# Dimension-major queries and keys for two narrow attentions, carried by DRAM into the rows that the scores contract over

## The reference

```
# block 4, self: 32 query heads, 8 key/value heads, causal
q = rope(x @ Wq); k = rope(x @ Wk); v = x @ Wv        # rope: first half of a head's 16 dims against the second
p = softmax(mask(q k^T) / 4);  x = layernorm(x + swapaxes(p v) @ Wo)
# block 5, cross: 32 query and 32 key heads over ctx of 256 positions x 256 features
q = axial_rope(x @ Wq, pos); k = axial_rope(ctx @ Wk, pos); v = ctx @ Wv   # even dims against odd dims
w = softmax(q k^T / 4);        x = layernorm(x + (w v) @ Wout + bout)
```

## Time and profile before

| | |
|---|---|
| median of 3 runs | 3688.03 us |
| the profiled execution's own time | 3694.4 us |
| its span, first to last instruction | 3692.8 us |
| TensorE busy over the span | 3308.8 us, 90% |
| VectorE, ScalarE, GpSimd | 2054.9 us, 1347.2 us, 565.8 us |
| mean granted TensorE clock | 0.935 |
| narrow attentions | from 1934.6 us (first weight load) to 2991.9 us (last norm) |

### The profile page before, as it was taken

The page is one execution under the profiler, slowest core; times in us unless marked ns, Lnnn a source line. Parts: engine busy times, 40 slices in busy tenths (PEclk is TensorE's granted clock), DMA queues, the critical chain, the costliest instruction groups (busy, mean ns, idle before and its releaser), DMA issues. The chain is left out here.

```text
span 3692.8 us, 54862 instructions
## 1 busy us (share of the span) xinstructions
PE 3308.8 (90%) x19817; PEld 2544.4 (69%) x19818; DVE 2054.9 (56%) x4982; ACT 1347.2 (36%) x2970; POOL 565.8 (15%) x621
## 2 busy tenths in 40 slices
PE   6999999999999999969937898889898857999995
PEld 6888888888888788854415555555555435787774
DVE  3555665566666666642154665666667645443445
ACT  0444434444444344432113343445445443122110
POOL 1333322222222222014140111210000000000000
PEclk7999999999999999979978999989999978999998
DMA  5111110110011011024340000000000011000001
GB/s 189 52 53 53 52 52 29 35 35 29 30 35 35 29 30 29 1 103 162 135 121 28 2 2 2 23 7 22 5 5 5 2 46 23 24 11 11 23 11 46
DMA packets 110614, 146.77 MB, mean 40 GB/s; under 512 B 23712, under 2 KB 72864, under 8 KB 109288
## 3 DMA queue, kind: packets, MB, share of 16 engines
q1 hardware_dynamic: 95904, 110.80, 9.3%
q0 software_dynamic: 14480, 32.91, 2.9%
HBM read 100.55 MB, written 42.08 MB: 39 GB/s over the span
## 5 line engine op out<-in xcount | busy, mean ns | idle before, releaser
L554 ACT ACTIVATE probs_w<-probs_w,low_w 128x256 f32<-128x256 f32 (+1 forms) x512 | 242.9, 475 | 589.6 <-DVE low_w L599 589.6
L1885 DVE TENSOR_REDUCE mx_n<-bank 128x6 f32<-128x768 f32 (+1 forms) x256 | 279.8, 1093 | 151.1 <-PE bank L1662 80.0
L1793 ACT ACTIVATE probsT_n<-bank 128x768 f32<-128x768 f32 (+1 forms) x256 | 235.7, 921 | 276.1 <-PE bank L1674 275.8
L572 DVE TENSOR_TENSOR probsT_lo_w<-bank,probsT_hi_w 128x384 fp32r<-128x384 f32 (+1 forms) x256 | 159.7, 624 | 124.8 <-ACT probsT_hi_w L537 124.0
L518 PE MATMUL bank<-wo_hi_w,oT_hi_w 128*128 128x512 f32 x512 | 211.6, 413 | 2.1 <-issue 2.1
L1656 PE MATMUL bank<-kT_n,qT_n 48*128 48x256 f32 (+1 forms) x1024 | 124.0, 322 | 93.7 <-DVE mx_n L1885 90.8
L518 PE MATMUL bank<-wo_hi_w,oT_lo_w 128*128 128x512 f32 x512 | 204.4, 399 | 0.0
L518 PE MATMUL bank<-wo_lo_w,oT_hi_w 128*128 128x512 f32 x512 | 204.2, 399 | 0.0
L582 DVE TENSOR_SCALAR probs_w<-probs_w,inv_w 128x256 f32<-128x256 f32 (+1 forms) x512 | 188.6, 411 | 20.8 <-issue 0.9
L450 PE MATMUL bank<-xT_lo_w,wq_hi_w 128*128 128x512 f32 x512 | 161.0, 396 | 0.0
L2323 DVE SCALAR_TENSOR_TENSOR h<-bank,scale_now,silu 128x512 f32<-128x512 f32 x64 | 48.0, 750 | 202.5 <-PE bank L2216 202.5
(11 more groups left out here) (368 smaller groups left out, 8190.3 us busy)
## 6 DMA issues: line engine op xcount, KB each, us to landing
expert_rows<-ctxT_hi_w SPq DMA_DIRECT2D x20, 512.0 KB, 4.5
work_m<-expert_rows SPq DMA_DIRECT2D x40, 256.0 KB, 2.6
expert_products<-work_m POOLq DMA_DIRECT2D x40, 256.0 KB, 2.6
staging_w<-in_L_attn_Wq SPq DMA_DIRECT2D x32, 256.0 KB, 3.0
expert_table<-ctxT_hi_w SPq DMA_DIRECT2D x16, 512.0 KB, 5.5
staging_w<-in_L_attn_Wo SPq DMA_DIRECT2D x32, 256.0 KB, 2.6
staging_w<-in_L_xattn_Wq SPq DMA_DIRECT2D x32, 256.0 KB, 2.7
staging_w<-in_L_xattn_Wo SPq DMA_DIRECT2D x32, 256.0 KB, 2.6
```

The costliest lines, as they stand in the source:

```text
L554: last = act.activation(pr, pr, ACT.Exp, bias=low[:, n % ROUNDS_OF_PROBS, tile:tile + 1], scale=-1.0, accum_out=den[:, n % ROUNDS_OF_PROBS ...
L572: return dve.tensor_tensor(dst, src, hi.bitcast(FP32), ALU.subtract)
L1793: act.activation(probsT[:, turn_ % SLOT_PAIRS, :, 0:cols], scoreT[:, :, 0:cols], ACT.Exp, scale=SCALE)\
L1885: dve.tensor_reduce(to.rearrange("p t h -> p h t"), seen, AX.X, ALU.max).then_inc(s["scores_read"], 1)
```

## The change

Queries and keys are projected with the weights as the stationary operand (`turned`), so that dimensions lie on the partitions and positions along the row, as the scores want them. ScalarE copies the product to `raw`. The rotation's partner dimension is now on the neighbouring partition (the self weights' columns are reordered once by ScalarE so that this holds there too), and SP fetches it with two DMAs to every second partition (`swap`). The tables of cosines and sines are transposed once per cross item (`table`) and once for all self items. VectorE rotates and splits the queries (`split_queries`, five instructions over 128 x 1024), GpSimd the keys (`split_keys`). SP stores both parts to DRAM (`store`, two DMAs each) and reads them back into the contraction rows (`place`, six DMAs of 16 partitions each for queries and for keys). An item is projected and split two iterations ahead and placed one iteration ahead. `parts`, `rotate` and the transposes `kT..`, `qT..` go.

```diff
-    before = [(x, 0) for x in ("xT0", "xT1", "k0", "k1", "kT00", "kT01", "kT10")]
+    before = [(x, 0) for x in ("table", "xT0", "xT1", "k0", "q0", "q1")]
...
+            def swap(name, n):
+                sp.wait_ge(s["prep_act"], uses.nth["q1" if name == "q" else k_uses(n)[-1], n])
+                chunks = DC if name == "q" else dims_chunks(n)
+                for i in range(2):
+                    sp.dma_start(swapped[name][i:P:2, 0:chunks, :], raw[name][1 - i:P:2, 0:chunks, :])\
...
+            def store(name, n):
+                sp.wait_ge(s[f"{name}_split"], n + 1)
...
+                for i, src in enumerate((hi[name].bitcast(FP32), raw[name])):
+                    sp.dma_start(bounce[name][i, 0:chunks, :, :].rearrange("c p t -> p c t"), src[:, 0:chunks, :])\
...
+            def place(name, n):
+                sp.wait_ge(s[f"{name}_stored"], 32 * (n + 1))
+                if n >= 2:
+                    sp.wait_ge(s["scoresT_ready"], 2 * PAIRS * (n - 1))
+                to = (qT if name == "q" else kT)[:, n % 2, :, :].bitcast(FP32)
+                for j, part in enumerate((0, 1, 0) if name == "q" else (0, 0, 1)):
                     for r in range(2):
+                        rows = slice(64 * r + HW * j, 64 * r + HW * j + HW)
...
+            for n in range(-1, ITEMS):
+                if n + 1 < ITEMS:
+                    place("k", n + 1)
+                    place("q", n + 1)
+                if n >= 0:
+                    negatives(1, n)
+                    negatives(2, n)
+                if n + 2 < ITEMS:
+                    swap("k", n + 2)
+                    swap("q", n + 2)
+                if n + 1 < ITEMS:
+                    negatives(0, n + 1)
+                if n + 2 < ITEMS:
+                    store("k", n + 2)
+                    store("q", n + 2)
...
+            def turned(b, n, w, src, chunk, chunks):
+                for cc in range(chunks):
+                    last = pe.matmul(b, w[:, cc, chunk * P:(chunk + 1) * P], src[:, cc, :], start=(cc == 0), stop=(cc == chunks - 1))
...
             def first_scores(n, pair):
-                if pair % 4 == 0:
-                    read(f"qT0{pair // 4}", n)
-                    read(f"qT1{pair // 4}", n)
+                if pair == 0:
+                    pe.wait_ge(s["k_placed"], 96 * (n + 1))
+                    pe.wait_ge(s["q_placed"], 96 * (n + 1))
...
+            def split_keys(n, part):
+                c = dims_chunks(n)
+                a, b, high = raw["k"][:, 0:c, :], swapped["k"][:, 0:c, :], hi["k"][:, 0:c, :]
...
+                if part == 0:
+                    pool.wait_ge(s["prep_act"], uses.nth["table", n if cross(n) else 0])
+                    pool.wait_ge(s["k_swapped"], 32 * (n + 1))
+                    pool.tensor_tensor(a, a, cos, ALU.mult)
...
+            def split_queries(n, part):
+                a, b, high = raw["q"][:, :, :], swapped["q"][:, :, :], hi["q"][:, :, :]
...
+                if part == 0:
+                    dve.wait_ge(s["prep_act"], uses.nth["table", n if cross(n) else 0])
+                    dve.wait_ge(s["q_swapped"], 32 * (n + 1))
+                    dve.tensor_tensor(a, a, cos, ALU.mult)
+                    dve.tensor_tensor(b, b, sin, ALU.mult)
+                elif part == 1:
+                    dve.tensor_tensor(a, a, b, ALU.add)
+                    dve.drain()
+                    dve.tensor_copy(high, a)
                 else:
+                    dve.tensor_tensor(a.bitcast(FP32R), a, high.bitcast(FP32), ALU.subtract).then_inc(s["q_split"], 1)
...
+                    if n + 2 < ITEMS and at in (13, 14, 15):
+                        split_queries(n + 2, at - 13)
```

More of the change, by code:

```diff
@@ L1408, in attention_narrow @@
     key_block = lambda n, h: h // 2 if cross(n) else h // 4
-    turns = lambda n: range(4 if cross(n) else 2)
+    k_uses = lambda n: ("k0", "k1") if cross(n) else ("k0",)
+    dims_chunks = lambda n: kv_heads(n) * HW // P
+    bounce = {name: nc.dram_tensor(f"{name}_parts", (2, DC, P, SEQ), FP32).ap() for name in "qk"}
     GROUPS = ((0, 6), (6, 10), (10, PAIRS))
@@ new lines, in negatives @@
+            def negatives(i, n):
+                name, (lo, hi_) = GROUP_NAMES[i], GROUPS[i]
+                sp.wait_ge(s["prep_act"], uses.nth[name, n])
+                for r in range(2):
+                    for l in range(2):
+                        row, at = 64 * r + ROWS + l, 16 * l + (hi_ - lo) * r
+                        sp.dma_start(qT[row:row + 1, n % 2, lo:hi_, :].bitcast(FP32),
+                                     negT[at:at + hi_ - lo, i, :].bitcast(FP32)).then_inc(s[f"{name}_there"], 16)
@@ new lines, in _ @@
+            for name in "kq":
+                swap(name, 0)
+            for name in "kq":
+                store(name, 0)
+            for n in range(-1, ITEMS):
[13 more added lines that the diff above has]
+                    store("q", n + 2)
@@ L1548, in _ @@
                 .then_inc(s["ctx_loaded"], 16)
[L1550 to L1553, removed]
+            nothing = pool.to_reg(0.0)
             def hide(n, pair):
@@ L1561, in hide, with spread_tables @@
                     .then_inc(s["hidden"], 1)
[L1563 to L1568, removed]
+            def spread_tables(n):
+                if n >= 1:
+                    pool.wait_ge(s["k_stored"], 32 * n)
+                for i in range(2):
+                    for t in range(TILES):
+                        to = spread[:, P * (TILES * i + t):P * (TILES * i + t + 1)].rearrange("p (h w) -> p h w", h=8)
+                        if cross(n):
+                            last = pool.tensor_copy(to, (rotary.cos, rotary.sin)[i][:, batch_of(n) * TILES + t, :]
+                                                    .unsqueeze(1).to_broadcast([P, 8, HW]))
+                        else:
+                            one = chip.const[:, (C_COS, C_SIN)[i] + HW * t:(C_COS, C_SIN)[i] + HW * (t + 1)]
+                            for a in range(2):
+                                last = pool.tensor_copy(to[:, :, a::2], one[:, 8 * a:8 * a + 8].unsqueeze(1).to_broadcast([P, 8, 8]))
+                last.then_inc(s["table_spread"], 1)
@@ L1615, in prepare @@
                     last = four(b, lambda i: ctx_sb[:, i % 2, i // 2 * P:(i // 2 + 1) * P])
+                elif name == "table":
+                    pe.wait_ge(s["table_spread"], max(n - BATCH + 2, 1))
+                    last = four(b, lambda i: spread[:, P * i:P * (i + 1)])
                 elif name in ("k0", "k1"):
@@ L1627, in prepare @@
                         read("xT1", n)
-                        pe.wait_ge(s["wq_cross_loaded" if cross(n) else "wq_loaded"], 16)
-                    last = project(b, xT, int(name[1]), wq, DIM, DC)
-                elif name[0:2] in ("kT", "qT"):
-                    t, n4 = int(name[2]), int(name[3])
-                    pe.wait_ge(s["split"], 4 * n + (0 if name[0] == "k" else 2) + t + 1)
-                    blocks = parts[:, t, :, :].rearrange("p (b two) w -> p b (two w)", two=2)
-                    last = four(b, lambda i: blocks[:, 4 * n4 + i, :])
+                        if cross(n):
+                            pe.wait_ge(s["wq_cross_loaded"], 16)
+                        else:
+                            pe.wait_ge(s["self_turned"], 2)
+                    for i in range(2):
+                        last = turned(b[:, i * SEQ:(i + 1) * SEQ], n, wq, xT, 2 * int(name[1]) + i, DC)
                 else:
@@ L1967, in _ @@
                 do(name, n)
+            for part in range(3):
+                split_queries(0, part)
             for n in range(-1, ITEMS):
```

190 lines of the change are left out of this document (90 added, 100 removed).

## The result

The changed kernel takes 3819.91 us (median of 4 runs, 3815.43 to 3826.95) where the kernel before takes 3690.85 us (4 runs, 3685.89 to 3694.96): the ratio is 1.0345, with a 95% interval of 1.0321 to 1.0368. It is slower by 3.45%, and 3824 us was forecast. The profiled execution has a span of 3825.3 us, 132.5 more than before; its last norm write in the stage stands at 3124.78 us instead of 2991.41, so all of it lies in the narrow attentions.

The account below looks back on a forecast made before the run. TensorE's program order was taken to bound the stage, VectorE close behind. Shorter iterations, outweighed by waits for negatives behind placements, plus start and GpSimd, added 136 us: 3824 us, own range 3750 to 3900, 8-in-10 range down to 3610.

Parts of the forecast that it names:

- The price of a placement: One DMA of 256 KB from DRAM into 16 partitions was put at 2.5 us, 1.25 for self keys.
- The first rival: Placements run at the fast rate, 1.3 us each, so TensorE waits 0.7 and 2 us: 3622 us; chance 0.20.
- the fast row: Lower bound for a placement: 4096 KB to all partitions landed in 20.9 us, 1.3 us per 256 KB.
- The halfway rival: Placements at 1.9 us, negatives at 24.4 (self) and 30.3 us (cross), total 3725 us; chance 0.09.
- SyncE's order: In SP's queue, group B's four negatives DMAs stand behind the queries' store and twelve placements, so they land late.
- The stall, cross: TensorE's wait for group B's negatives at step 6 of a cross iteration: needed at 21, landed at 37.5, 16.5 us.
- Self: The same wait for negatives in a self iteration: needed at 18.5, landed at 30, 11.5 us.
- The sign of 10 to 17 us at pair 6: Profile sign: second scores at pair 6 wait 10 to 17 us for negatives in iterations 0 to 14, more in cross.
- Iterations without DMA trouble: Iteration times from engine work alone: self 60.3 - 7.2 = 53.1 us, cross 66.8 - 9.0 = 57.8 us.
- GpSimd: GpSimd's key splits beside VectorE's norm and split: 2 us in each of six cross iterations, 12 us together.
- The start: First scores at about 1995 instead of 1963.3 us, then 24 instead of 21 us to first second scores: 34 us.
- The swap's wait: Swap issued only after step 11's last query projection: about 1 us of wait beyond step 12, within an unchanged sum.

Follow-up runs that it names:

- half_placed: The changed kernel, with each placement from the third item on carrying only the first half of its heads, same DMAs and order: 3637.55 us, 0.9847 of the kernel before.
- the probe: The changed kernel plus nine groups of four DMAs of about 256 KB into differently placed partitions behind its narrow attentions: 3884.38 us, groups included.
- negb_before_queries: The changed kernel, with SyncE issuing group B's four negatives DMAs between the keys' and the queries' placements: 3667.18 us, 0.9925 of the kernel before.
- half_placed_no_key_split: The kernel with half-size placements, with GpSimd's split of cross items' keys left out but for one tiny instruction: 3619.32 us, 0.9806 of the kernel before.

## Why the prediction was right

The sum, by second scores at the start and norm writes after it; an iteration stands in the distance in which its stall falls:

| | predicted | measured |
|---|---|---|
| start | +34 | +36.4 |
| seven self iterations (0 to 6) | +30 | +33.7 |
| iteration 7 | +9 | +11.0 |
| six cross iterations (8 to 13) | +45 | +46.6 |
| iterations 14 and 15 | +6 | +5.8 |
| GpSimd beside VectorE, cross iterations | +12 | in the rows above |
| together | +136 | +133.5 |

- **The price of a placement**, 2.5 us between 1.3 and 2.6: 2.34 us. The first rival (1.3) fell; half_placed has its time, 3638 against 3622. The reason given, sixteen partitions as an eighth of what the fast row wrote to, is not the right one: the probe shows that it is where they lie and not how many they are. The halfway rival fell too (its 24.4 adds up to 24.6).
- **SyncE's order.** The chain of store, twelve placements and negatives is the one in the timeline. negb_before_queries shows that it decides.
- **The stall, cross:** needed at 21 us (the terms given add up to 21.6), there at 37.5; measured 22.8 and 37.6. **Self:** needed at 18.5, there at 30; measured 21.0 (2208.11 to the stall at 2229.1) and 28.0, a stall of 7.0 us where 11.5 was worked out. The sign of 10 to 17 us at pair 6 came true from iteration 7 on (13.0 to 14.9); in iterations 1 to 6 it was 6.2 to 8.5. The term was too large there, and the self iterations came out right (64.6) by luck: without the stall they are 54.6 us and not 53.1, and a term was missing, since at the lower clock TensorE's matmuls take 4.7 us longer in the self window and 3.4 in the cross window. The working had no clock in it at all.
- **Iterations without DMA trouble:** 53.1 and 57.8 worked out; half_placed has 54.6 and 58.1, half_placed_no_key_split 56.4 for cross. The 53.1 started from 60.3 us, an average with iteration 7 in it; from the 59.8 of the self iterations alone the gain was 5.2 us, not 7.2.
- **GpSimd:** 2 us in each of six iterations worked out; 18 us in all without the stall, 1.7 to 3.3 an iteration. It was counted for too few: keys of cross items are split two items ahead, so iterations 6 and 7 bear it too. The instructions that it holds up most in cross iterations are the norm write's, which have one tensor input and per-row scalars, not two tensors; two inputs in SBUF, as the prediction had it, show in iterations 6 and 7. What it adds in the changed kernel itself, beside the stall, was not measured.
- **The start:** first scores at 1995 worked out, 1994.79 measured; from there to the first second scores 25.9 us instead of 24.
- **The swap's wait** of about 1 us did not show: VectorE's split waited for the swap at the start only.

The mechanism, its place and its price held. That the total came within 4 us is luck in part. GpSimd's 12 us belong to the cross iterations: with them and iteration 7 these were forecast at +66 and measured at +57.6, and all the others, the start included, were forecast at +70 and measured at +75.9. Not tried: a layout in which the sixteen rows lie evenly over the ports (steps of four do, but 48 rows then don't stay together), and a shorter start.

## What to carry to other kernels

Before a small DMA that TensorE waits for is put behind a block of large ones in program order, work out when the block's data end, not when its issues do; moving one call was worth 4% here, and a queue of its own for the small DMA two thirds of that. Ask of a DMA into few partitions where these lie: the same 256 KB cost 2.34 us in sixteen adjacent rows and 1.6 in rows in steps of three. And a stall has a second price, the lower clock behind it, which belongs into the sum.

## What was not expected of the hardware

- A DMA with an outermost index of three kept three DMA engines busy (share 0.19), at 57 GB/s together, 19 for each; sixteen engines into sixteen adjacent rows reach 7 GB/s each.
- Small DMAs from a queue of their own began to move 10.6 to 11.5 us after their first issue while the other queue was full of placements, however many of these were still to land, and after 1.2 us where there were none.
- GpSimd's two-input instructions stretched VectorE's tensor_scalar from SBUF to SBUF (two of 128x512) from 0.99 to 3.95 us and a tensor_tensor with both inputs in SBUF from 1.22 to 3.37 us, and did not touch its maxima out of PSUM.
